# Local attention on TensorE: the input of the tile after next is turned ahead of the first turn of the probabilities

## The chip, the core and the metric

The kernel runs on one core of a Trainium2 chip. The metric is the device time of one execution in microseconds (us); several runs are given by their median.

## What is computed

The reference is four blocks, one after the other, each added to its input, over 4 x 1024 tokens of 256 channels: an attention with ALiBi, a local-attention transformer of two layers, a Mamba scan and a mixture of 32 experts. The change lies in the local attention. Cut to what matters, one layer of it is:

```python
h = shift_token(x)                       # second half of the channels comes from the token before
q, k, v = split(h @ wqkv)                # 8 heads of 64
q = rotary(l2norm(q) * qs); k = rotary(l2norm(k) * ksc)
sim = einsum('bhwid,bhwjd->bhwij', 8 * q, look_around(k))   # blocks of 128 tokens, own block and the one before
attn = softmax(where(mask, -max, sim))
o = einsum('bhwij,bhwjd->bhwid', attn, look_around(v))
x = x + o @ wo                           # then the gated feed-forward of the layer
```

## The kernel before, in words

The program is a row of phases: A and B for the first attention, then twice (layer 0 and layer 1) the phase D for the local attention and the phase E for its feed-forward, and F, H and I for the rest. Phase D is the function `phase_window`. It goes over 32 tiles of 128 tokens, with one instruction stream for each engine, written out by hand in the order in which the engine takes it; semaphores tie the streams together. Nothing reorders them.

For a tile i, whose pass is one turn of the loop at the end of the function:

- TensorE multiplies q and k to scores (`score`, L1380), in two halves of four heads.
- VectorE adds the mask and takes the maximum of each half (`maxima`, L1216 and L1219); ScalarE takes the exponentials of each half (`exps`, L1298) and signals `exped` after each.
- TensorE meanwhile projects q and k of tile i+1 (`project_qk`, L1353). It then turns the probabilities, first half (`turn_p(i, 0)`, L1390, eight transposes), projects v of tile i+1 (`project_v`, L1360), turns the input of tile i+2 (`turn_h`, L1345 and L1346, two transposes into the PSUM tile `p_hz`), and turns the second half of the probabilities (`turn_p(i, 1)`, L1390 again).
- Then come the turned reciprocals of the sums (`spread_inv`, L1413), the product with v (`weigh`, L1403), the turns of the rotated k and q of tile i+1 (`turn_qk`, L1370) and the output projection (`project_z`, L1421), on which VectorE's `residual` (L1241) waits. ScalarE copies the turned input to `hT` (`put_hT`, L1273) late in its own pass, behind both halves of the probabilities.
- Between the exponentials and the output projection VectorE inverts the sums (L1225), rotates and sums k and q of tile i+1 (L1186 to L1202) and divides the weighted values (`divide`, L1235, tile `yT`).

The input of a tile comes by two transfers, `LA_base` (L3170) and `LA_before` (L3175), into one of four buffers. SyncE (its DMA queue is SPq) issues them in the same stream as the stores of the results, and once per layer the loads for phase E (`feed.load`, L3224 to L3253: 24 transfers of weights, biases and the first two chunks of tokens) stand in that stream too:

```python
            for i in range(TILES):
                if i + 3 < TILES:
                    load(i + 3)
                sp.wait_ge(z1_ready, i + 1)
                sp.dma_start(T["z1"][i * P + 1:(i + 1) * P + 1, :], z1[:, i % 2, :]).then_inc(stored[i % 2], 16)
                if i == TILES // 2:
                    ...
                    feed.load(sp, T, layer)
```

So tile 20's input is issued in the turn i = 17 of this loop, behind the whole of `feed.load`, and `turn_h(20)` stands in TensorE's pass of tile 18.

Of the kernel before, what the change touches and what calls it, by code (L numbers as in the profile page):

```python
# [18 lines left out]
TILES = TOKENS // P  # L19
# [1005 lines left out]
def phase_window(nc, T, layer, local, feed):  # L1025
    with ExitStack() as ctx:
# [75 lines left out]
        def reached(eng, sem, value):  # L1102
            if value > 0:
                eng.wait_ge(sem, value)
# [235 lines left out]
        def _(pe):  # L1340
            def turn_h(i):
                pe.wait_ge(local.loaded[i % 4], 16 * local.loads(layer, i))
                reached(pe, hT_ready, i)
                reached(pe, z1_ready, i - 2)
                nc.tensor.transpose(p_h[:, 0:P], base[:, i % 4, 0:P], ident[:, :])  # L1345
                nc.tensor.transpose(p_h[:, P:2 * P], before[:, i % 4, :], ident[:, :]).then_inc(h_turned, 1)  # L1346

            def project_qk(i):
                pe.wait_ge(hT_ready, i + 1)
                reached(pe, qkT_ready, i)  # L1350
                for m in (1, 0):
                    for k in range(KD):
                        last = nc.tensor.matmul(p_qk[:, m, :], hT[:, i % 2, k, :],  # L1353
                                                wqkv[:, k, m * INNER:(m + 1) * INNER], start=k == 0, stop=k == KD - 1)
                    last.then_inc(qk_done, 1)

            def project_v(i):
                reached(pe, v_ready, i)
                for k in range(KD):
                    last = nc.tensor.matmul(p_v[:, :], hT[:, i % 2, k, :], wqkv[:, k, 2 * INNER:3 * INNER],  # L1360
                                            start=k == 0, stop=k == KD - 1)
                last.then_inc(v_done, 1)

            def turn_qk(i):
                pe.wait_ge(k_rotated, i + 1)
                for n, src in ((1, kr), (0, qr)):
                    if n == 0:
                        pe.wait_ge(q_rotated, i + 1)
                    for t in range(PAIRS):
                        last = nc.tensor.transpose(p_qk[:, n, t * P:(t + 1) * P],  # L1370
                                                   src[:, 2 * t:2 * t + 2, :].rearrange("p a b -> p (a b)"), ident[:, :])
                last.then_inc(qk_turned, 1)

            def score(i):
                pe.wait_ge(qkT_ready, i + 1)
                reached(pe, yT_ready, i)
                for n in range(2):
                    for m in range(4 * n, 4 * n + 4):
                        strip = slice(LD * (m % 2), LD * (m % 2) + LD)
                        last = nc.tensor.matmul(scores[:, place[m], :, :].rearrange("p a b -> p (a b)"),  # L1380
                                                qkT[strip, 0, m // 2, i % 2, :],
                                                qkT[strip, 1, m // 2, :, :].rearrange("p a b -> p (a b)"),
                                                start=True, stop=True)
                    last.then_inc(scored, 1)

            def turn_p(i, n):
                pe.wait_ge(exped, 2 * i + n + 1)
                for m in range(4 * n, 4 * n + 4):
                    for s in range(2):
                        last = nc.tensor.transpose(scores[:, m, s, :], probs[:, m, s, :], ident[:, :])  # L1390
                last.then_inc(p_turned, 1)

            def weigh(i, half):
                if half == 0:
                    pe.wait_ge(pT_first, i + 1)
                    pe.wait_ge(v_ready, i + 1)
                else:
                    pe.wait_ge(pT_second, i + 1)
                for t in range(2 * half, 2 * half + 2):
                    for s in range(2):  # L1400
                        for e in range(2):
                            n = 2 * t + e
                            last = nc.tensor.matmul(p_y[LD * e:LD * e + LD, t * P:(t + 1) * P],  # L1403
                                                    v[:, s, n * LD:(n + 1) * LD], pT[:, place[n], s, :],
                                                    start=s == 0, stop=s == 1, tile_position=(0, LD * e))
                if half == 1:
                    last.then_inc(weighted, 1)

            def spread_inv(i):
                pe.wait_ge(wide_ready, i + 1)  # L1410
                pe.wait_ge(pT_first, i + 1)
                for t in range(PAIRS):
                    last = nc.tensor.transpose(p_inv[:, t * P:(t + 1) * P],  # L1413
                                               inv_wide[:, 2 * t:2 * t + 2, :].rearrange("p e d -> p (e d)"), ident[:, :])
                last.then_inc(inv_spread, 1)

            def project_z(i):
                pe.wait_ge(yT_ready, i + 1)
                reached(pe, hT_ready, min(i + 3, TILES))
                for t in range(PAIRS):  # L1420
                    last = nc.tensor.matmul(p_z, yT[:, t, :], wo[:, t, :], start=t == 0, stop=t == PAIRS - 1)  # L1421
                last.then_inc(projected, 1)
# [8 lines left out]
            for i in range(TILES):  # L1431
                score(i)
                if i + 1 < TILES:
                    project_qk(i + 1)
                turn_p(i, 0)
                if i + 1 < TILES:
                    project_v(i + 1)
                if i + 2 < TILES:
                    turn_h(i + 2)
                turn_p(i, 1)  # L1440
                spread_inv(i)
                weigh(i, 0)
                weigh(i, 1)
                if i + 1 < TILES:
                    turn_qk(i + 1)
                project_z(i)
# [1850 lines left out]
```

## Time and profile before

| | before |
|---|---|
| median of 3 runs | 3570.31 us (3567.07 to 3571.28) |
| the profiled execution, its own time | 3574.62 us |
| its span, first to last instruction | 3572.8 us |
| mean granted TensorE clock | 0.953 |
| phase D, layer 0 and layer 1 | about 753 to 1249 us and 1515 to 2008 us |

A row of a timeline gives start and length in us, the engine, the line of the kernel, the operation, the output and the input by their names in the program, the number of instructions merged, and in brackets how long the engine sat idle before it and what ended that. PE is TensorE's matmul side and PEld its weight loads, which run under the matmuls. In float32 a product is recorded as two matmuls, a transpose as one. Matmul lengths contain the pipeline's latency, so starts are the safer thing to subtract.

### The profile page before, as it was taken

The page shows a single profiled execution, that of the slowest core. Times are in us where ns is not written, and L with a number is a line of the kernel's source. Part 1 is how long each engine was busy: PE and PEld are TensorE (multiplying, and loading weights), DVE is VectorE, ACT ScalarE, POOL GpSimd, SP SyncE. Part 2 cuts the span into 40 slices and gives each one's busy share as a digit, 9 for nine tenths or more (in the row PEclk, how much of TensorE's full clock was granted, in tenths as well). Part 3 has the DMA queues.
Part 4 walks back from the last instruction along what each step waited for, and adds up shares of the span by engine and source line. Part 5 has one row for each costly group of instructions (what it writes and reads, how often), then busy time and mean ns, then how long its engine had stood idle before and what let it go on. Part 6 is the DMA issues. An engine that isn't in the chain of part 4 may idle for free. (4 is left out here: it accounts for less than half of the span.)

```text
span 3572.8 us, 52196 instructions
## 1 busy us (share of the span) xinstructions
PE 3193.6 (89%) x18048; PEld 1967.1 (55%) x18048; DVE 2458.4 (69%) x4614; ACT 1846.8 (52%) x3942; POOL 1411.3 (40%) x967
## 2 busy tenths in 40 slices
PE   8599999979999989999999899898388888888878
PEld 5244444346666645566666555433156555555777
DVE  8488887647777632277777433379699999999543
ACT  2177767736666611156666311165467777777111
POOL 4201111132222211132222211133499999999433
PEclk9699999989999999999999899999599999999989
DMA  5945657110020043000020123134444252420776
GB/s 165 168 57 91 88 86 133 35 35 23 23 66 23 14 171 99 26 19 24 22 67 21 37 68 91 48 138 149 164 170 177 82 177 86 173 93 36 260 264 219
DMA packets 263746, 347.27 MB, mean 97 GB/s; under 512 B 70619, under 2 KB 183241, under 8 KB 262844
## 3 DMA queue, kind: packets, MB, share of 16 engines
q1 hardware_dynamic: 249572, 308.29, 31.0%
q10 hardware_dynamic: 9432, 23.35, 1.9%
q0 software_dynamic: 4480, 12.30, 0.9%
q8 instruction: 144, 2.36, 0.3%
q14 instruction: 118, 0.97, 0.1%
HBM read 227.72 MB, written 112.80 MB: 95 GB/s over the span
## 5 line engine op out<-in xcount | busy, mean ns | idle before, releaser
L2411 POOL TENSOR_TENSOR H_feed<-H_ndu,H_bs 128x1024 f32<-128x1024 f32 x256 | 595.0, 2364 | 6.1 <-DMA H_bs<-between_bc 3.2
L888 ACT ACTIVATE B_probs<-B_p_exp,B_key_bias 128x512 f32<-128x512 f32 (+3 forms) x768 | 394.2, 582 | 161.8 <-PE B_p_exp L950 131.3
L779 DVE TENSOR_REDUCE B_part_max<-B_p_max 128x1 f32<-128x512 f32 (+3 forms) x768 | 374.3, 544 | 82.2 <-PE B_p_max L914 79.7
L1298 ACT ACTIVATE D_probs<-D_scores,D_neg,D_rq 128x256 f32<-128x256 f32 x512 | 282.9, 574 | 255.2 <-DVE D_neg L1219 255.2
L2382 ACT ACTIVATE H_decay<-H_ndt,H_rate 128x1024 f32<-128x1024 f32 x256 | 287.8, 1125 | 195.7 <-DVE H_turning L2464 103.5
L1662 PE MATMUL E_p_ag<-E_hT,FA_w 128*128 128x512 f32 x640 | 283.2, 602 | 1.9 <-ACT E_hT L1618 1.9
L911 PE MATMUL B_p_max<-B_k,B_q 100*128 100x512 bf16 (+3 forms) x768 | 256.8, 341 | 29.7 <-DMA B_q<-in_q_rows 19.7
L947 PE MATMUL B_p_exp<-B_q,B_k 100*128 100x512 bf16 (+3 forms) x768 | 250.4, 330 | 24.8 <-DMA B_q<-B_shift_rows 18.0
L2464 DVE TENSOR_TENSOR_SCAN H_turning<-H_decay,H_feed 128x1024 f32<-128x1024 f32 x112 | 253.4, 2274 | 20.6 <-POOL H_feed L2411 18.3
L2515 PEld LDWEIGHTS H_p_y<-H_minus,H_sT 128*128 128x128 f32 x1792 | 225.3, 200 | 76.0 <-ACT H_sT L2367 56.0
L2515 PE MATMUL H_p_y<-H_minus,H_sT 128*128 128x128 f32 x1792 | 233.7, 287 | 35.5 <-ACT H_sT L2367 35.5
L1634 ACT ACTIVATE E_gated<-E_p_ag,FA_b 128x512 f32<-128x512 f32 x96 | 62.5, 651 | 372.9 <-PE E_p_ag L1662 353.7
L1156 POOL TENSOR_TENSOR D_rnorm<-D_norm,D_power 128x8 f32<-128x8 f32 x64 | 106.1, 1657 | 375.0 <-DVE D_norm L1174 375.0
L2367 ACT ACTIVATE H_sT<-H_p_T,H_cT 128x128 f32<-128x128 f32 x896 | 242.3, 387 | 14.3 <-PE H_p_T L2505 14.0
L1353 PE MATMUL D_p_qk<-LA_wqkv,D_hT 128*128 128x512 f32 x512 | 241.5, 615 | 0.9 <-ACT D_hT L1273 0.9
L1216 DVE CUSTOM_DVE_ANT_0 D_scores<-D_scores,D_mask 128x256 f32<-128x256 f32 x512 | 201.7, 456 | 55.5 <-PE D_scores L1380 55.3
L2464 DVE TENSOR_TENSOR_SCAN H_decay<-H_decay,H_feed 128x1024 f32<-128x1024 f32 x96 | 218.9, 2280 | 14.4 <-POOL H_feed L2411 14.3
L1160 POOL TENSOR_TENSOR D_rnorm<-D_norm,D_power 128x8 f32<-128x8 f32 x64 | 106.6, 1666 | 288.9 <-DVE D_norm L1174 288.9
L1662 PEld LDWEIGHTS E_p_ag<-E_hT,FA_w 128*128 128x128 f32 x640 | 121.9, 193 | 155.3 <-issue 151.6
L1589 DVE SCALAR_TENSOR_TENSOR E_act_out<-E_p_ag,FA_b,E_gated 128x512 f32<-128x512 f32 x96 | 67.8, 706 | 198.8 <-ACT E_gated L1634 198.8
L2523 PE MATMUL H_p_y<-H_part,H_minus 128*128 128x512 f32 x384 | 186.0, 607 | 8.4 <-DVE H_part L2440 8.4
L911 PEld LDWEIGHTS B_p_max<-B_k,B_q 100*128 100x128 bf16 x768 | 75.2, 98 | 207.7 <-DVE B_part_max L779 131.5
(276 smaller groups left out, 6798.5 us busy)
## 6 DMA issues: line engine op xcount, KB each, us to landing
H_bs<-between_bc SPq DMA_DIRECT2D x64, 512.0 KB, 8.1
H_cs<-between_bc SPq DMA_DIRECT2D x36, 512.0 KB, 8.7
B_q<-between_q_parts SPq DMA_DIRECT2D x90, 128.0 KB
B_k<-between_k_parts SPq DMA_DIRECT2D x90, 128.0 KB
between_slots_x<-E_clear ACTq DMA_DIRECT2D x4, 2570.0 KB, 19.2
I_xe<-between_slots_x ACTq DMA_DIRECT2D x32, 257.0 KB, 6.4
LA_base<-between_z SPq DMA_DIRECT2D x64, 128.0 KB, 2.2
between_z<-D_z SPq DMA_DIRECT2D x64, 128.0 KB
```

What stands on the lines that cost most here:

```text
L779: nc.vector.reduce_max(part_max[:, g % 2, kc, qb, h:h + 1], p_max[:, use % 3, 0:keys], AX.X).then_inc(maxed, 1)
L888: nc.scalar.activation(probs[:, x % PROBS, skip:512], p_exp[:, n % SCORES, skip:512], ACT.Exp, bias=key_bias[:, g % SETS, kb - 4 * Q + 4, ...
L911: last = nc.tensor.matmul(p_max[:, use % 3, 0:keys], q[0:KR, u, h, qb * P:(qb + 1) * P], k[0:KR, u, h, 512 * kc:512 * kc + keys], start=Tr ...
L947: last = nc.tensor.matmul(p_exp[:, n % SCORES, skip:512], k[0:KR, u, h, kb * P:(kb + 1) * P], q[0:KR, u, h, 512 * Q + skip:512 * Q + 512], ...
L1298: last = nc.scalar.activation(probs[:, place[m], :, :].rearrange("p a b -> p (a b)"), scores[:, place[m], :, :].rearrange("p a b -> p (a b ...
L1353: last = nc.tensor.matmul(p_qk[:, m, :], hT[:, i % 2, k, :], wqkv[:, k, m * INNER:(m + 1) * INNER], start=k == 0, stop=k == KD - 1)
L1662: last = nc.tensor.matmul(p_ag[:, m % 2, n, :], w1[:, k, at:at + P], hT[:, i % 2, k, :], **flags)
L2367: last = nc.scalar.activation(sT[:, k % 2, h * HB + b, :], p_T[:, h, b, :], ACT.Copy, scale=cT[:, i % 2, h * HB + b, s:s + 1])
L2382: nc.scalar.activation(decay[:, n % 2, :], ndt[:, g % 2, :], ACT.Exp, scale=rate[:, m, s:s + 1]).then_inc(decayed, 1)
L2411: nc.gpsimd.tensor_tensor(feed[:, n % AHEAD, :], ndu[:, g % 2, :], bs[:, s, :], ALU.mult).then_inc(fed, 1)
L2464: nc.vector.tensor_tensor_scan(out, decay[:, n % 2, :], feed[:, n % AHEAD, :], 0.0, ALU.mult, ALU.add).then_inc(scanned, 1)
L2515: last = nc.tensor.matmul(p_y[:, h, b * P:(b + 1) * P], sT[:, k % 2, h * HB + b, :], minus[:, :], start=False, stop=False)
```

## The change

The two turns of the input of tile i+2 move from behind v's projection to ahead of the first turn of the probabilities. Nothing is added or removed; the other engines' streams are the same.

```diff
                 score(i)
                 if i + 1 < TILES:
                     project_qk(i + 1)
+                if i + 2 < TILES:
+                    turn_h(i + 2)
                 turn_p(i, 0)
                 if i + 1 < TILES:
                     project_v(i + 1)
-                if i + 2 < TILES:
-                    turn_h(i + 2)
                 turn_p(i, 1)
                 spread_inv(i)
                 weigh(i, 0)
```

TensorE's stream, one pass of a tile in phase D before the change:

```order
L1380 MATMUL D_scores<-D_qkT 128x256 x8
L1353 MATMUL D_p_qk<-LA_wqkv,D_hT 128x512 x4
L1390 MATMUL D_scores<-LA_ident,D_probs 128x128 x8
L1360 MATMUL D_p_v<-LA_wqkv,D_hT 128x512 x2
L1345 MATMUL D_p_hz<-LA_ident,LA_base 128x128
L1346 MATMUL D_p_hz<-LA_ident,LA_before 128x128
L1390 MATMUL D_scores<-LA_ident,D_probs 128x128 x8
L1413 MATMUL D_scores<-LA_ident,D_inv_wide 128x128 x4
L1403 MATMUL D_scores<-D_pT,D_v 64x128 x16
L1370 MATMUL D_p_qk<-LA_ident,D_kr 128x128 x4
L1370 MATMUL D_p_qk<-LA_ident,D_qr 128x128 x4
L1421 MATMUL D_p_hz<-LA_wo,D_yT 128x256 x4
```

Of the ten transposes and one projection between `project_qk` and the second turn of the probabilities, L1345 and L1346 are the last. The same engine and the same pass after the change:

```order
L1380 MATMUL D_scores<-D_qkT 128x256 x8
L1353 MATMUL D_p_qk<-LA_wqkv,D_hT 128x512 x4
L1345 MATMUL D_p_hz<-LA_ident,LA_base 128x128
L1346 MATMUL D_p_hz<-LA_ident,LA_before 128x128
L1390 MATMUL D_scores<-LA_ident,D_probs 128x128 x8
L1360 MATMUL D_p_v<-LA_wqkv,D_hT 128x512 x2
L1390 MATMUL D_scores<-LA_ident,D_probs 128x128 x8
```

L1345 and L1346 have moved up past eight turns of the probabilities (L1390) and the projection of v (L1360), and now stand ahead of both. They wait for three things: the transfers of tile i+2, the copy of tile i+1's turned input (`hT_ready`), and the residual of tile i-1 (`z1_ready`).

## Rows read from the trace of the kernel before

**Rows 1.** The page's first part, busy time of each engine over the span

```profile
PE 3193.6 (89%) x18048; PEld 1967.1 (55%) x18048; DVE 2458.4 (69%) x4614; ACT 1846.8 (52%) x3942; POOL 1411.3 (40%) x967
```

**Rows 2.** Timeline of PE in an ordinary pass, tile 17 of layer 0

```profile
1021.50 2.00 PE L1380 MATMUL D_scores<-D_qkT 64*128 64x256 f32 x16
...
1027.03 1.09 PE L1390 MATMUL D_scores<-LA_ident,D_probs 128*128 128x128 f32 x8
1027.96 1.88 PE L1360 MATMUL D_p_v<-LA_wqkv,D_hT 128*128 128x512 f32 x4
1029.68 0.27 PE L1345 MATMUL D_p_hz<-LA_ident,LA_base 128*128 128x128 f32 x1
...
1029.90 1.04 PE L1390 MATMUL D_scores<-LA_ident,D_probs 128*128 128x128 f32 x8
...
1031.30 1.97 PE L1403 MATMUL D_scores<-D_pT,D_v 128*64 128x128 f32 x32
...
1036.37 2.00 PE L1380 MATMUL D_scores<-D_qkT 64*128 64x256 f32 x16
```

**Rows 3.** Timeline of all engines, another ordinary pass: five of its waits

```profile
905.40 0.56 ACT L1298 ACTIVATE D_probs<-D_scores,D_neg,D_rq 128x256 f32<-128x256 f32 x1 [4.00 <-DVE D_neg L1219]
...
907.74 0.86 PEld L1390 LDWEIGHTS D_scores<-LA_ident,D_probs 128*128 128x128 f32 x8 [0.73 <-ACT D_probs L1298]
...
910.47 0.20 DVE L1225 RECIPROCAL D_inv<-D_total 128x8 f32<-128x8 f32 x1 [0.31 <-ACT D_probs L1298]
...
914.55 0.42 PEld L1370 LDWEIGHTS D_p_qk<-LA_ident,D_qr 128*128 128x128 f32 x4 [0.23 <-DVE D_qr L1196]
...
915.15 1.59 PEld L1421 LDWEIGHTS D_p_hz<-LA_wo,D_yT 128*128 128x128 f32 x8 [0.18 <-DVE D_yT L1235]
```

**Rows 4.** Timeline of PE, the pass of tile 18 of layer 0

```profile
1046.54 0.33 PE L1345 MATMUL D_p_hz<-LA_ident,LA_base 128*128 128x128 f32 x1 [1.84 <-DMA LA_before<-between_z]
...
1046.82 1.04 PE L1390 MATMUL D_scores<-LA_ident,D_probs 128*128 128x128 f32 x8
...
1052.90 2.00 PE L1380 MATMUL D_scores<-D_qkT 64*128 64x256 f32 x16
```

**Rows 5.** Timeline of PE, the pass of tile 18 of layer 1

```profile
1797.43 2.00 PE L1380 MATMUL D_scores<-D_qkT 64*128 64x256 f32 x16
...
1806.74 0.33 PE L1345 MATMUL D_p_hz<-LA_ident,LA_base 128*128 128x128 f32 x1 [0.96 <-DMA LA_before<-between_z]
...
1813.10 2.00 PE L1380 MATMUL D_scores<-D_qkT 64*128 64x256 f32 x16
```

**Rows 6.** Timeline of SyncE's queue around `feed.load`, layer 0

```profile
1022.55 1.37 SPq L3238 DMA_DIRECT2D FA_ident<-in_ident  x1
...
1034.21 5.98 SPq L3228 DMA_DIRECT2D FA_h<-between_z  x1
...
1041.56 0.77 SPq L3170 DMA_DIRECT2D LA_base<-between_z  x1
1042.70 0.34 SPq L3175 DMA_DIRECT2D LA_before<-between_z  x1
```

**Rows 7.** All transfers of LA_before, us from issue to landing

```profile
DMA to landing us min/median/max: 1.8/2.0/6.2
```

**Rows 8.** Timeline of PE, tile 31 of layer 0, the last

```profile
1237.22 1.09 PE L1390 MATMUL D_scores<-LA_ident,D_probs 128*128 128x128 f32 x8 [3.53 <-ACT D_probs L1298]
1239.41 1.97 PE L1390 MATMUL D_scores<-LA_ident,D_probs 128*128 128x128 f32 x8 [1.09 <-ACT D_probs L1298]
...
1242.16 3.48 PE L1403 MATMUL D_scores<-D_pT,D_v 128*64 128x128 f32 x32
```

**Rows 9.** Stretches: length; busy us of five engines; then granted clock, DMA share, GB/s

```profile
586.50:589.90 3.40, 3.20 (x8) 2.60 (x9) 0.00 (x0) 0.00 (x0) 0.00 (x0) 0.51 0.06 14
1038.30:1052.90 14.60, 12.76 (x84) 8.47 (x82) 9.96 (x30) 9.74 (x24) 3.39 (x3) 1.00 0.41 112
...
1239.40:1245.20 5.80, 5.79 (x40) 5.46 (x42) 0.62 (x2) 2.36 (x3) 0.00 (x0) 0.50 0.00 0
```

## The prediction

> **What bounds the kernel now.** The page's first part comes first, and it can mislead here: TensorE is busy for 89% of the span [rows 1], so any pause taken out of it looks like a gain. The timeline of one ordinary pass of phase D says otherwise. From one `score` to the next, 1021.50 to 1036.37, it is 14.87 us [rows 2], and PE shows no idle row in between. But matmul lengths are modelled, and the weight loads show four short waits, each on another engine [rows 3]. Followed round the pass, they close a ring: ScalarE sits 4.00 us until VectorE has the first maxima; VectorE waits 0.31 us for the last exponentials and starts the reciprocal at 910.47; from there it works through seven more operations; the turn of q waits 0.23 us for VectorE's `qr`, and the output projection 0.18 us for VectorE's `yT`. The projection leads to the next `score`, the score to the maxima, these to the exponentials. What TensorE does between `project_qk` and `turn_qk`, which is where the change lies, is beside this ring: it only has to be done by the time VectorE wants the weighted values.
>
> How much slack it has there is read from the two passes in which it was late. I looked for passes longer than 14.87 us and found two in which `turn_h` waits for a transfer: tile 18 of layer 0, 1036.37 to 1052.90, 16.53 us, where L1345 sat until LA_before had landed [rows 2, 4], and tile 18 of layer 1, 1797.43 to 1813.10, 15.67 us, the same wait [rows 5]. In an ordinary pass L1345 starts 8.18 us after `score` (1021.50 to 1029.68) [rows 2]. In these two it started 10.17 and 9.31 us after, so 1.99 and 1.13 us late, while the passes grew by 1.66 and 0.80 us. Both differences are 0.33 us: that is the slack.
>
> Why the transfer is late stands in SyncE's queue: `feed.load` begins at 1022.55 and the input of tile 20 is issued only at 1041.56 (LA_base) and 1042.70 (LA_before), 19 us later, one of the issues alone taking 5.98 us [rows 6]. In an ordinary pass the input was issued a whole pass before it is wanted.
>
> **The change, part by part.** It moves 60 pairs of transposes (30 tiles in each layer's loop) past `turn_p(i, 0)` and `project_v`. No instruction is added and no transfer moves in its queue.
>
> 1. *Ordinary passes, 58 of 60.* The pair takes 0.22 us (1029.68 to 1029.90) [rows 2]. At the new place the first turn of the probabilities waits for ScalarE anyway, since its weight load had been idle for 0.73 us [rows 3]; most of the 0.22 us goes into that wait. The second turn of the probabilities then comes up to 0.15 us earlier, or the first about 0.1 us later, and both ends lie beside the ring: on one side ScalarE copies the first turned half only after the last exponentials (by program order), on the other `qr` and `yT` come when VectorE has them. The slack of 0.33 us covers 0.22 us even if no part of it is hidden. Cost taken: 0. Bounds: a loss of 0, by this slack; a gain of 0.22 us x 60 = 13.2 us if I am wrong about the ring and the whole pair vanished from the path (the rival below).
>
> 2. *The two late passes.* Now `turn_h(20)` waits for the same transfer 2.65 us earlier in the stream (1027.03 to 1029.68, `turn_p(i, 0)` 0.93 and `project_v` 1.72) [rows 2]. The landing does not move, for SyncE's issues depend on the residuals of tiles 16 and 17, which are past. But behind the wait there now stand `turn_p(18, 0)` and `project_v(19)`, which before were done while the transfer was under way. They run after the landing and push everything behind them by their 2.65 us: second turn of the probabilities, weighing, `yT`, output projection. There is no slack left, it was used up already. Nothing else is late first: ScalarE's copies wait for the same turns. So 2 x 2.65 = 5.3 us. This does not depend on how late the transfer is, as long as it comes later than the old place plus 0.33 us; if it came earlier by all of 1.66 and 0.80 us, the loss would still be 2.65 each. It falls to zero only for a transfer that lands 4.3 and 3.5 us sooner than here.
>
> The transfer's lateness is where a page can be weighed. LA_before landed, by PE's waking at 1046.54, 3.84 us after the start of its issue at 1042.70, while the median of all is 2.0 [rows 4, 6, 7]. The Trainium skill, DMA: Bandwidth & Descriptors, section "Anatomy of one DMA — SWDGE (gpsimd) path", puts the fixed cost of a transfer at about 2.0 us, an estimate by which it would land at 1044.7, 2.8 us after the new place and hardly late at the old one; the loss would be 2.8 - 0.33 = 2.5 us for the layer in place of 2.65. The trace disagrees with 2.0 for this transfer, which shares the engines with the 24 of `feed.load`, and I go by the trace.
>
> 3. *TensorE's clock.* The new waits are long: from the new place (5.53 us after `score`, so 1041.90 and 1802.96) [rows 2, 5] to the landings at 1046.54 and 1806.74 it is 4.64 and 3.78 us [rows 4, 5]. Before, it was 1.84 and 0.96 us, and the granted clock stayed at 1.00, 2.4 GHz, in that stretch [rows 9]. After 3.53 us of idle time in tile 31 it did not: the turns and the weighing behind it took 1.97 and 3.48 us, where an ordinary pass has 1.04 and 1.97, and the granted clock was 0.50, 1.2 GHz [rows 2, 8, 9]. Both new waits are longer than 3.53 us, so I expect the lower clock behind both. Its price: in tile 31 from the second turn at 1239.41 to the end of the weighing at 1245.64 it took 6.23 us, against 3.37 us in an ordinary pass (1029.90 to 1033.27), 2.9 us lost [rows 2, 8]. A short low stretch elsewhere was 3.4 us long [rows 9], which would lose half of that, 1.7 us. What follows the landing is some 6 us of TensorE work without a pause, all of it on the path; tile 31 had a second pause of 1.09 us, so I go near the short one, 1.9 us, 3.8 for both layers. Bounds: 0 (the clock holds, as after 1.84 us) and 2 x 2.9 = 5.8 us.
>
> The Trainium skill, TensorE: Matmul & The Clock Gate, section "What's actually happening", says that the low rate is the default and activity releases it, so a long wait is paid twice, once as the wait and once behind it. By that the sum is 5.3 + 3.8; without it 5.3. Tile 31's rows agree with it.
>
> The sum is 0 + 5.3 + 3.8 = 9.1 us. The profiled execution took 3574.6 us and would take 3583.7. It is 4.3 us above the median of the runs shown; since the waits are paid in every run, the 9.1 us go on the median: 3570.3 + 9.1 = **3579.4 us**.
>
> **The rivals.** Changes under 0.2%, 7.1 us, are about what a measurement of this kernel can't tell from none.
>
> - *The wait blocks, the clock holds.* For it: in tile 31 of layer 0 the idle stretch was followed by a second pause, which tile 18 has not. Against it: both new waits are longer than 3.53 us. 5.3 us more, 3575.6; with one low stretch in two, 3577.5. Chance 0.20.
> - *The transfer is in time in an ordinary run.* The queue may be quicker where no profile is taken. It needs a landing 3.5 to 4.3 us sooner, and 5.98 us of the delay is one issue that waits for the queue itself [rows 6]. 3570.3. Chance 0.07.
> - *Faster: TensorE is the bound after all.* The 89% [rows 1] and the missing idle rows speak for it. Then the pair vanishes into the wait ahead of the first turn, up to 13.2 us less, against 9.1 more: 3566.2. It decides if more than 9.1 / 60 = 0.15 us per pass is on the path. Against it: the waits for `qr` and `yT` [rows 3], and that in tile 18 a delay of 1.99 us grew the pass by only 1.66. Chance 0.04.
> - *Both low stretches are long*, 2.9 us each or more, or a second transfer is late too (tile 21's, issued 2 to 3 us behind tile 20's, and wanted one pass later, so hardly): 5.3 + 5.8 = 11.1, 3581.4 and above. Chance 0.09.
>
> **How the numbers follow.** The forecast has 0.60; its own range, 1.2 to 2.7 us for each low stretch, is 7.7 to 10.7 us more, 3578.0 to 3581.0. The range for 8 in 10 takes in the 5.3 us of the first rival less a microsecond for the runs' spread, and the long low stretches: 3574.3 to 3582.6. Slower by over 7.1 us: nearly all of the forecast (0.55) and the last rival, 0.63. Within: the first two rivals and what is left of the forecast, 0.33. Faster: 0.04.
>
> **What would show it.** In the profile after, passes of phase D other than tile 18's should still be 14.87 us, with `qr` and `yT` as releasers of the same short waits; the wait of the first turn of the probabilities on the exponentials should be gone or much shorter. In tile 18 of both layers L1345 should stand directly behind L1353, with an idle time near 4.6 and 3.8 us that LA_before ends, and the passes should be near 21.1 and 20.2 us (16.53 and 15.67 + 2.65 + 1.9). The granted clock behind the landing should read 0.5 for a few us. I am wrong if the ordinary passes have changed by 0.02 us or more, if LA_before lands sooner, or if nothing behind it is slower.

## The result, and the profile after

| | before | after |
|---|---|---|
| median of 22 runs each | 3572.71 us (3567.07 to 3578.58) | 3579.85 us (3573.18 to 3590.42) |
| ratio to before, 95% interval | | 1.0024 (1.0017 to 1.0030) |
| the profiled execution, its own time | 3574.62 us | 3590.42 us |
| mean granted TensorE clock | 0.953 | 0.953 |

The changed kernel is slower by 0.24%, 8.6 us by the ratio (6.1 to 10.7 by its interval); the difference of the two medians is 7.1 us. The profiled execution after is the longest of the 22, 10.6 us above their median, and of its distance to the one before, 15.8 us, a part has nothing to do with the change: phase D's first matmul starts at 758.30 us, where it started at about 753, so some 5.5 us were gone before the first changed instruction. So passes are compared here, and not spans.

The timeline of PE in the kernel after, an ordinary pass (tile 17 of layer 0, as in [rows 2]):

```profile
1025.90 2.00 PE L1380 MATMUL D_scores<-D_qkT 64*128 64x256 f32 x16
...
1031.37 0.27 PE L1345 MATMUL D_p_hz<-LA_ident,LA_base 128*128 128x128 f32 x1
...
1031.59 1.04 PE L1390 MATMUL D_scores<-LA_ident,D_probs 128*128 128x128 f32 x8
1032.46 1.88 PE L1360 MATMUL D_p_v<-LA_wqkv,D_hT 128*128 128x512 f32 x4
1034.18 1.04 PE L1390 MATMUL D_scores<-LA_ident,D_probs 128*128 128x128 f32 x8
```

and the weight loads (PEld) of the same pass, with what ended their idle time:

```profile
1031.48 0.91 PEld L1390 LDWEIGHTS D_scores<-LA_ident,D_probs 128*128 128x128 f32 x8
...
1034.12 0.86 PEld L1390 LDWEIGHTS D_scores<-LA_ident,D_probs 128*128 128x128 f32 x8 [0.60 <-ACT D_probs L1298]
...
1038.26 0.42 PEld L1370 LDWEIGHTS D_p_qk<-LA_ident,D_qr 128*128 128x128 f32 x4 [0.27 <-DVE D_qr L1196]
1038.86 1.59 PEld L1421 LDWEIGHTS D_p_hz<-LA_wo,D_yT 128*128 128x128 f32 x8 [0.19 <-DVE D_yT L1235]
```

The first turn of the probabilities waits for nothing now, 5.69 us after `score` in place of 5.53 [rows 2]; the second starts 8.28 us after it in place of 8.40, and it now has the wait on the exponentials, 0.60 us. The waits for `qr` and `yT` are where they were in [rows 3]. So the stretch was rearranged within its slack, and the next `score` came at 1040.79, after 14.89 us, where it was 14.87. The pair takes 0.22 us and pushed the first turn back by 0.16, so only 0.06 us of it was hidden in a wait.

Tile 18 of layer 0, the same view of the kernel after, to set against [rows 4]:

```profile
1040.79 2.00 PE L1380 MATMUL D_scores<-D_qkT 64*128 64x256 f32 x16
1042.71 3.70 PE L1353 MATMUL D_p_qk<-LA_wqkv,D_hT 128*128 128x512 f32 x8
1052.10 0.48 PE L1345 MATMUL D_p_hz<-LA_ident,LA_base 128*128 128x128 f32 x1 [5.69 <-DMA LA_before<-between_z]
...
1052.59 1.91 PE L1390 MATMUL D_scores<-LA_ident,D_probs 128*128 128x128 f32 x8
1054.29 2.42 PE L1360 MATMUL D_p_v<-LA_wqkv,D_hT 128*128 128x512 f32 x4
1056.56 1.04 PE L1390 MATMUL D_scores<-LA_ident,D_probs 128*128 128x128 f32 x8
...
1062.64 2.00 PE L1380 MATMUL D_scores<-D_qkT 64*128 64x256 f32 x16
```

and of layer 1, against [rows 5]:

```profile
1808.55 2.00 PE L1380 MATMUL D_scores<-D_qkT 64*128 64x256 f32 x16
...
1817.62 0.48 PE L1345 MATMUL D_p_hz<-LA_ident,LA_base 128*128 128x128 f32 x1 [3.44 <-DMA LA_before<-between_z]
...
1818.10 1.91 PE L1390 MATMUL D_scores<-LA_ident,D_probs 128*128 128x128 f32 x8
1819.81 3.62 PE L1360 MATMUL D_p_v<-LA_wqkv,D_hT 128*128 128x512 f32 x4
...
1829.39 1.78 PE L1380 MATMUL D_scores<-D_qkT 64*128 64x256 f32 x14
```

The passes are 21.85 and 20.84 us, against 16.53 and 15.67: 5.3 and 5.2 us more, 10.5 in all. Two pieces can be told apart by splitting each pass at the landing, which is where L1345 starts. From the landing to the next scores it was 6.36 us in both layers before; now it is 10.54 and 11.77. In front of the landing it was 10.17 and 9.31 us and is 11.31 and 9.07, so 1.14 us more and 0.24 us less, and that is the transfer's own scatter. In layer 0 SyncE issued LA_before 20.2 us after it had begun `feed.load` before the change, and 21.5 us after it in this execution:

```profile
1026.96 0.33 SPq L3238 DMA_DIRECT2D FA_ident<-in_ident  x1
...
1048.41 0.34 SPq L3175 DMA_DIRECT2D LA_before<-between_z  x1
```

The stretches of the kernel after, in the columns of [rows 9], show the clock in the waits and behind the landings:

```profile
1046.40:1048.40 2.00, 0.01 (x1) 0.00 (x0) 1.61 (x4) 2.00 (x8) 0.84 (x1) 1.00 0.80 232
1048.70:1052.10 3.40, 0.00 (x0) 0.00 (x0) 1.96 (x5) 0.25 (x2) 0.95 (x2) 0.50 0.73 216
1052.10:1055.30 3.20, 3.20 (x12) 2.68 (x13) 0.00 (x0) 0.76 (x1) 0.00 (x0) 0.50 0.01 2
1055.50:1062.60 7.10, 7.10 (x63) 5.59 (x61) 3.33 (x6) 3.93 (x7) 1.26 (x1) 1.00 0.01 2
1814.20:1816.40 2.20, 0.00 (x0) 0.00 (x0) 1.85 (x4) 2.20 (x8) 1.07 (x1) 1.00 1.03 304
1816.70:1817.60 0.90, 0.00 (x0) 0.00 (x0) 0.75 (x3) 0.01 (x1) 0.72 (x2) 0.50 0.29 86
1817.60:1823.30 5.70, 5.68 (x15) 3.51 (x16) 2.77 (x6) 1.51 (x2) 0.00 (x0) 0.50 0.00 1
1823.50:1829.30 5.80, 5.80 (x60) 5.06 (x58) 1.53 (x3) 3.38 (x5) 1.21 (x1) 1.00 0.01 1
```

In both layers the granted clock falls to 0.50, 1.2 GHz, while TensorE still waits, and it stays there for about 6.8 us: from 1048.6 to 1055.4 in layer 0, and from 1816.6 to 1823.4 in layer 1. What differs is where the landing falls in that stretch. In layer 0 the first 3.5 us of it lie in the wait and 3.3 us behind the landing; in layer 1 it is 1.1 and 5.8 us. Behind the landing TensorE is full of work, and then it is at 2.4 GHz again. In the rows of the passes the eight transposes take 1.91 us there and 1.04 us later.

### The profile page after: what moved, and what is told of

Same layout as the page of the kernel before. It is cut to its first block and busy times, and to the rows that moved or that the text cites. A ratio compares the mean times of both kernels' runs of the same rounds, so it can differ in the third digit from the quotient of the medians.

```text
span 3588.6 us, 52196 instructions
## 1 busy us (share of the span) xinstructions
PE 3191.9 (89%) x18048; PEld 1964.3 (55%) x18048; DVE 2459.4 (69%) x4614; ACT 1847.6 (51%) x3942; POOL 1413.5 (39%) x967
## 5 line engine op out<-in xcount | busy, mean ns | idle before, releaser
L2523 PE MATMUL H_p_y<-H_part,H_minus 128*128 128x512 f32 x384 | 184.5, 603 | 10.8 <-DVE H_part L2440 10.7
```

## The experiments

My theory: all of the loss lies in tile 18's two passes, and has two parts, the work that now stands behind the wait (2.65 us each) and the lower clock that comes with the longer idle time. The rivals: the loss is spread over the ordinary passes; TensorE is the bound; the rest beside the blocked work is only a later landing.

### The two kinds of pass taken apart

The new place in all passes but tile 18's:

```diff
+                if i + 2 < TILES and (i != TILES // 2 + 2):
+                    turn_h(i + 2)
                 turn_p(i, 0)
...
+                if i + 2 < TILES and not (i != TILES // 2 + 2):
+                    turn_h(i + 2)
                 turn_p(i, 1)
```

> The changed order in every pass but tile 18's, which keeps the old place. My theory (the whole loss is in the two late passes): ordinary passes 14.87 us, tile 18's 15.7 to 16.9 us as before the change, time that of the kernel before within 2 us. Rival (the loss is spread over the ordinary passes, 8.6 / 60 = 0.14 us each): passes of about 15.0 us and some 8 us slower than before.

Measured: 3571.35 us against 3571.78 of before, ratio 1.0002 (0.9990 to 1.0014). The pass of tile 18 in layer 0, timeline of PE:

```profile
1037.50 2.00 PE L1380 MATMUL D_scores<-D_qkT 64*128 64x256 f32 x16
...
1046.75 0.33 PE L1345 MATMUL D_p_hz<-LA_ident,LA_base 128*128 128x128 f32 x1 [0.91 <-DMA LA_before<-between_z]
...
1053.12 1.13 PE L1380 MATMUL D_scores<-D_qkT 64*128 64x256 f32 x8
```

15.62 us, and 6.37 from landing to scores, as before the change. In layer 1 it was 15.25 us. The other 58 moved pairs cost nothing that can be measured. The other way round, only tile 18's pass has the new place. Of the two conditions of the edit above the first is shown; the second is its opposite, as above:

```diff
-                if i + 2 < TILES and (i != TILES // 2 + 2):
+                if i + 2 < TILES and (i == TILES // 2 + 2):
```

> The old order in every pass but tile 18's, which alone has the new place: one pass of 32 in each layer. My theory: all of the loss, 5.3 us of blocked work and 2 to 6 us of lower clock, so 7 to 11 us slower than before, tile 18's passes 20 to 22 us. Rival (spread over the passes): 0.3 us slower.

Measured: 3578.27 us, 6.5 above before by medians; ratio 1.0011 (0.9999 to 1.0022), which is 3.9 us with an interval from -0.4 to 7.9. By the ratio that is less than the 7 to 11 us expected, which its interval only touches, and in time alone this run doesn't rule out the rival's 0.3 us. Its profile does: the pass of layer 0 is 20.98 us, and that of layer 1,

```profile
1797.74 2.00 PE L1380 MATMUL D_scores<-D_qkT 64*128 64x256 f32 x16
1806.31 0.48 PE L1345 MATMUL D_p_hz<-LA_ident,LA_base 128*128 128x128 f32 x1 [2.95 <-DMA LA_before<-between_z]
...
1818.23 1.13 PE L1380 MATMUL D_scores<-D_qkT 64*128 64x256 f32 x8
```

is 20.49 us, 11.92 of it from landing to scores. From landing to scores it is 10.64 us in layer 0. Tile 18's passes have grown about as in the full change, and the others are 14.87 to 14.89 us, or within 0.02 us of what they were before where they were longer.

### The late transfer removed

SyncE issues tile 20's input ahead of the loads for phase E. The same edit was made on the changed order, and then on the order before:

```diff
-                if i + 3 < TILES:
+                if i + 3 < TILES and i != TILES // 2 + 1:
                     load(i + 3)
...
                 if i == TILES // 2:
+                    load(i + 4)
                     sp.wait_ge(first_row, 16)
```

> The changed order, and SyncE issues the input of tile 20 ahead of the loads for phase E in place of behind them. My theory: no pass waits for a transfer, tile 18's are 14.87 us, the granted clock stays at 1.00 there; the loss of 9 is gone and also the 2.5 us that the kernel before still paid: 2 to 3 us faster than before. Rival (the landing is slow by the load on the engines, not by the queue): the wait stays and the time is 5 us or more above before.

> The order before, with the input of tile 20 issued ahead of the loads for phase E. My theory: 2.5 us faster than before (1.66 and 0.80 us of the two passes) and within 1 us of the same edit on the changed order: with the transfer in time, the place of the turns is worth nothing. Rival (the new place gains in the ordinary passes, hidden by the late ones): the changed order is the faster of the two by several us.

Measured: 3569.56 us, ratio 0.9992 (0.9981 to 1.0002), and 3568.30 us, ratio 0.9985 (0.9973 to 0.9997), against the same 3571.78. Tile 18's pass in layer 0, timeline of PE, first with the new place:

```profile
1037.59 2.00 PE L1381 MATMUL D_scores<-D_qkT 64*128 64x256 f32 x16
...
1043.05 0.27 PE L1346 MATMUL D_p_hz<-LA_ident,LA_base 128*128 128x128 f32 x1
...
1052.47 0.92 PE L1381 MATMUL D_scores<-D_qkT 64*128 64x256 f32 x6
```

then with the old one:

```profile
1029.31 2.00 PE L1381 MATMUL D_scores<-D_qkT 64*128 64x256 f32 x16
...
1037.49 0.27 PE L1346 MATMUL D_p_hz<-LA_ident,LA_base 128*128 128x128 f32 x1
...
1044.19 1.14 PE L1381 MATMUL D_scores<-D_qkT 64*128 64x256 f32 x8
```

Both are 14.88 us, and so are the passes of layer 1. With the transfer in time no idle row is left and the place of the two turns is worth nothing; the intervals of the two kernels overlap widely. So the input's place behind `feed.load` in SyncE's stream made it late. How much of that is the queue's 19 us and how much the slower landing behind the other transfers (3.84 us from issue, where the median is 2.0) these two runs don't part. By its time alone the first isn't clear of no change, for its interval takes in 1. The second of the two is faster than both given kernels, by 5.4 us or 0.15%, with 2.4 us of it seen in the passes (1.65 and 0.79); the ratio's interval, 1.1 to 9.6 us, takes that in.

### The clock apart from the blocked work

On the changed order, four more products stand ahead of the two turns, in tile 18's pass alone. Their result is overwritten by v's projection, so nothing computed changes:

```diff
+            def fill(i):
+                reached(pe, v_ready, i)
+                for n in range(4):
+                    nc.tensor.matmul(p_v[:, :], hT[:, i % 2, n % 2, :], wqkv[:, n % 2, 2 * INNER:3 * INNER],
+                                     start=True, stop=True)
...
+                if i == TILES // 2 + 2:
+                    fill(i + 1)
                 if i + 2 < TILES:
                     turn_h(i + 2)
                 turn_p(i, 0)
```

> The changed order, with four more products of the input with v's weights in tile 18's pass ahead of the two turns, 3.4 us of work whose result v's projection overwrites. My theory (two parts: blocked work and clock): the granted clock stays at 1.00 behind the landing, from the landing to the next scores it takes 9.0 us (6.36 + 2.65) and not 10.5 or more, and the loss against before falls from about 9 to about 5 us. Rival (the clock has no part, the rest is a later landing): no difference from the changed kernel, or slower by the added work.

Measured: 3576.66 us against 3571.05 of before, ratio 1.0011 (1.0000 to 1.0021). Tile 18 of layer 0 and of layer 1, timeline of PE:

```profile
1054.53 0.33 PE L1345 MATMUL D_p_hz<-LA_ident,LA_base 128*128 128x128 f32 x1 [2.01 <-DMA LA_before<-between_z]
...
1063.49 1.35 PE L1386 MATMUL D_scores<-D_qkT 64*128 64x256 f32 x10
...
1816.71 0.27 PE L1345 MATMUL D_p_hz<-LA_ident,LA_base 128*128 128x128 f32 x1
...
1825.61 1.35 PE L1386 MATMUL D_scores<-D_qkT 64*128 64x256 f32 x10
```

and the same two stretches with their clock:

```profile
1054.60:1063.50 8.90, 8.90 (x76) 7.06 (x76) 3.33 (x6) 4.89 (x7) 1.31 (x1) 1.00 0.01 3
1816.70:1825.60 8.90, 8.90 (x75) 7.07 (x74) 4.66 (x9) 4.89 (x7) 1.43 (x2) 1.00 0.01 3
```

From the start of L1345 to the next scores it is 8.96 and 8.90 us at a granted clock of 1.00, where the changed kernel had 10.54 and 11.77. In layer 0 TensorE still waited 2.01 us for the transfer; in layer 1 L1345 followed the four products without an idle row, so there the wait was filled whole, and its start is not the landing. So the lower clock costs 1.6 and 2.9 us there, and the blocked work is what is left over 6.36: 2.6 and 2.5 us. More work, in a wait, made the kernel no slower and the passes shorter (20.03 and 17.80 us). That the whole kernel is faster than the changed one doesn't follow from the times (the intervals overlap); the passes show it.

### Less work behind the wait

The two turns behind the first turn of the probabilities and ahead of v's projection, in every pass, against the kernel before:

```diff
                 turn_p(i, 0)
+                if i + 2 < TILES:
+                    turn_h(i + 2)
                 if i + 1 < TILES:
                     project_v(i + 1)
-                if i + 2 < TILES:
-                    turn_h(i + 2)
```

> The two turns stand between the first turn of the probabilities and v's projection: only the projection, 1.72 us, is queued behind the wait. My theory: 1.72 us of blocked work in each late pass in place of 2.65, so 3.4 us, and the lower clock behind waits of about 3.7 and 2.9 us in one or both layers (1.5 to 3 us): 3.4 to 8 us slower than before. Ordinary passes 14.87 us. Rival (any place ahead of v costs the same): as the changed kernel, 8 to 9 us.

Measured: 3575.74 us, ratio 1.0011 (1.0003 to 1.0020), 3.9 us slower (1.1 to 7.1). Tile 18 of layer 0, timeline of PE, and below it the stretch behind the landing:

```profile
1044.90 0.33 PE L1345 MATMUL D_p_hz<-LA_ident,LA_base 128*128 128x128 f32 x1 [3.78 <-DMA LA_before<-between_z]
...
1045.22 3.53 PE L1360 MATMUL D_p_v<-LA_wqkv,D_hT 128*128 128x512 f32 x4
...
1054.68 0.92 PE L1380 MATMUL D_scores<-D_qkT 64*128 64x256 f32 x6
```

```profile
1045.00:1048.40 3.40, 3.40 (x6) 1.47 (x7) 1.76 (x4) 0.00 (x0) 0.00 (x0) 0.52 0.02 6
```

9.78 us from landing to scores. That is 6.36, and 1.72 for the projection of v, and 1.70, half of the 3.4 us at the lower clock: the two prices add up to the measured one. The cost follows the amount of work that stands behind the wait. In layer 1 it was 9.76 us, and there the clock fell only 1.2 us after the landing at 1808.52, with TensorE at work:

```profile
1808.60:1809.50 0.90, 0.90 (x4) 0.58 (x5) 0.90 (x2) 0.00 (x0) 0.00 (x0) 1.00 0.02 7
1809.80:1813.00 3.20, 3.20 (x11) 2.06 (x10) 1.32 (x3) 0.00 (x0) 0.00 (x0) 0.50 0.00 0
```

The three kernels with a low stretch in tile 18's passes, side by side, in us. The bounds of a stretch are read from the granted clock in steps of 0.3 us. The last column is the time from landing to scores, less 6.36 and the blocked work by the rows before (2.65, or 1.72 in this last run):

| run, layer | idle before the landing | clock low for | of that behind the landing | half of it | landing to scores | left for the clock |
|---|---|---|---|---|---|---|
| after, 0 | 5.69 | 6.8 | 3.3 | 1.6 | 10.54 | 1.5 |
| after, 1 | 3.44 | 6.8 | 5.8 | 2.9 | 11.77 | 2.8 |
| tile 18's pass alone, 0 | 4.72 | 3.4 | 3.4 | 1.7 | 10.64 | 1.6 |
| tile 18's pass alone, 1 | 2.95 | 6.8 | 6.1 | 3.0 | 11.92 | 2.9 |
| ahead of v's projection, 0 | 3.78 | 3.4 | 3.4 | 1.7 | 9.78 | 1.7 |
| ahead of v's projection, 1 | 3.03 | 3.4 | 3.4 | 1.7 | 9.76 | 1.7 |

In all six the price is half of the low stretch that lies behind the landing, to 0.1 us. (With the 2.6 and 2.5 us of blocked work found with the filled wait, the first two rows read 1.6 and 2.9.) It doesn't follow the length of the idle time.

### How much slack TensorE has

The order before, with the two turns of every tile done k times into the same place:

```diff
-                nc.tensor.transpose(p_h[:, 0:P], base[:, i % 4, 0:P], ident[:, :])
-                nc.tensor.transpose(p_h[:, P:2 * P], before[:, i % 4, :], ident[:, :]).then_inc(h_turned, 1)
+                for n in range(k):
+                    nc.tensor.transpose(p_h[:, 0:P], base[:, i % 4, 0:P], ident[:, :])
+                    last = nc.tensor.transpose(p_h[:, P:2 * P], before[:, i % 4, :], ident[:, :])
+                last.then_inc(h_turned, 1)
```

> The order before, with both turns of the input done twice into the same place in every pass: 0.22 us more TensorE work in each. My theory (TensorE has 0.33 us of slack beside the ring): ordinary passes stay at 14.87 to 14.90 us, time within 2 us of before. Rival (TensorE is the bound): 0.22 us more in each pass, 15.09 us, 14 us slower.

> The same with both turns done four times, 0.65 us more in each pass. My theory: the slack of 0.33 us is used up and 0.32 us per pass shows, passes of 15.19 us, 60 x 0.32 = 19 us slower than before. Rival (TensorE is the bound): passes of 15.5 us, 40 us slower. If the slack is larger than I read it, nothing shows.

Measured: twice, 3572.78 us, ratio 1.0003 (0.9994 to 1.0013); four times, 3588.60 us, ratio 1.0049 (1.0034 to 1.0064), 17.5 us. An ordinary pass with the turns twice, between the starts of two `score`:

```profile
1107.05 2.00 PE L1382 MATMUL D_scores<-D_qkT 64*128 64x256 f32 x16
...
1121.93 2.00 PE L1382 MATMUL D_scores<-D_qkT 64*128 64x256 f32 x16
```

and with the turns four times:

```profile
1103.79 2.00 PE L1382 MATMUL D_scores<-D_qkT 64*128 64x256 f32 x16
...
1118.94 2.00 PE L1382 MATMUL D_scores<-D_qkT 64*128 64x256 f32 x16
```

14.88 and 15.15 us. 0.22 us more work on a TensorE that looks 89% busy cost nothing, and of 0.65 us (six transposes of 0.11) 0.28 showed over 14.87: the slack is 0.37 us. I had read 0.33 from the two late passes. In tile 18's passes of the last run, where the transfer was waited for, it was 7.02 us from the landing to the next scores, 6.36 and all of the added 0.66: nothing of it was hidden behind the wait.

## Why the prediction was right

- *Ordinary passes, cost 0.* Right. The changed order with tile 18 left out measured 1.0002. A few ordinary passes are 15.1 to 15.2 us, and they are so before and after. The 29 passes of each layer but the first and tile 18's take 863.6 us in all before, both layers together, and 864.1 after; the order before with the input issued early has 864.1 as well, so the 0.5 us are no cost of the place. TensorE as the bound falls with the doubled turns. One step of the reasoning was wrong without harm: most of the pair's 0.22 us was to go into the wait of the first turn of the probabilities, but that wait is one of the weight loads, under matmuls that were still running, and only 0.06 us was hidden there. The slack covered the rest, as the prediction had said it could.
- *Blocked work, 2 x 2.65 us.* Right: 2.6 and 2.5 us with the clock held at 1.00, and 1.72 where only v's projection is behind the wait.
- *The clock, 2 x 1.9 us.* The mechanism was right and the sum near: 1.6 and 2.9 us, 4.5 in place of 3.8. A single price for both layers was too simple, and that their sum was near is in part luck. I had taken a short low stretch, 3.4 us, all of it behind the landing. In the changed kernel both stretches were 6.8 us long, and layer 0 was cheap only because half of its stretch lay in the wait. I had not reckoned with where the landing falls in the stretch. My bound of 2.9 us for one held just in this execution; in the run with tile 18's pass alone it was 2.9 to 3.0.
- *The landing doesn't move.* Right as to the change, since SyncE's issues hang on earlier tiles: from issue to landing it was 3.84 us before and 3.69 after in layer 0. But its scatter from one execution to the next, 1.1 us in layer 0, is as large as a term of the sum; I had not put it into the range by itself. It does explain why the pass after was 21.85 us where I had written near 21.1: 1.1 of it is the landing, and the blocked work and the clock came to 4.2 in place of 4.55 us.
- *The sum.* 9.1 us forecast; 8.6 us by the ratio, 7.1 by the medians. By the passes of this one execution it is 10.5, of which 0.9 is the landing, so 9.6. Two slips of the prediction's own sums change nothing: 5.3 us less one give 3574.6 and not 3574.3 for the lower end, and 0.55 and 0.09 add up to 0.64 and not 0.63. That the transfer would be in time without a profile was argued against with the one issue of 5.98 us; what that issue waits for no run shows.
- *The transfer's fixed cost by the Trainium skill.* The section that the prediction names, in DMA: Bandwidth & Descriptors, gives its figure for transfers that GpSimd issues. This one is SyncE's, though the median here is 2.0 us too. With 2.0 us for this transfer the loss without the clock would have come to 2.5 us in layer 0 and, by the issue at 1803.08, to 1.8 us in layer 1. The idle times, 5.69 and 3.44 us as measured, would have come out near 2.8 and 2.1, and no run here shows a fall of the clock behind one of 2.1 us. LA_before was waited for 3.7 us after its issue in the trace after too (1048.41 to 1052.10).

What isn't shown: the share of the lower clock in the time of the whole kernel. The run with the filled wait is nearer to before than the changed kernel is (1.0011 against 1.0024), but their intervals overlap. The tile's two passes, each of one profiled execution, also grew by more than the time did: by 9.3 us in the run with tile 18's pass alone (20.98 and 20.49 us against 16.53 and 15.67) and by 7.4 us in the one with the turns ahead of v's projection (20.19 and 19.42), where both ratios give 3.9 us, with intervals that end at 7.9 and 7.1. A part can be where the landing fell in these few executions; the rest stays open. Nor is it shown what decides when the clock falls in a wait, or for how long; the table gives six cases, all of single executions.

## What to carry to other kernels

When an instruction that waits for a transfer is moved earlier on an engine that takes its work in order, look for the few turns of the loop in which that transfer is late, and charge everything that it was moved past, in each of them; the ordinary turns may say nothing at all. A share of busy time near 90% doesn't make an engine the bound: follow the short waits round one turn of the loop and see whether they close without it. And where such a turn waits because its transfer is queued behind a bulk load, try issuing it ahead of that load: here that was worth more than any place of the instruction. Where a wait is long enough for the clock to fall, the price is half of what is left of the low stretch when the work comes back, and so it can differ between two waits that look alike.

## What I had not expected of the hardware

The granted clock fell in a wait of 2.95 us (layer 1 of the run with tile 18's pass alone changed) and held over the 2.01 us in the run with the filled wait. It didn't fall at a fixed time after the work had stopped: 2.2 and 2.4 us after it in the kernel after, but 5.2 us in layer 0 of the run with tile 18's pass alone, and 4.2 us in layer 1 of the last placement, when TensorE had been at work again for 1.2 us. Low stretches of 3.4 and of 6.8 us both occurred. In the kernel after both were 6.8 us, and still one cost 1.6 us and the other 2.9, because a part of the first lay in the wait, where it costs nothing.
